# A selective scan on one core: the low half of the x-projection split moves from VectorE to GpSimd

## The chip, the cores and the metric

One Trainium2 chip, one core. The metric is the device time of one execution, in microseconds (us), and smaller is better. TensorE multiplies matrices into the banks of the accumulator memory (PSUM), ScalarE and VectorE read and write both PSUM and the state memory (SBUF), GpSimd reads and writes SBUF only, and SyncE issues the transfers. In the rows the engines are PE (matmul), PEld (weight load), DVE (VectorE), ACT (ScalarE), POOL (GpSimd) and SP (SyncE).

## What is computed

Two layers over x of 8 images, 192 channels and 64 by 64 positions. The second is a non-local attention block, which the change leaves alone. The first, cut to what matters:

```python
xn = _ln_cf(x, ln_w, ln_b)
xc, z = jnp.split(jnp.einsum('dc,bchw->bdhw', in_proj_w, xn), 2, axis=1)
xc = silu(depthwise_conv3x3(xc) + conv_b)
xs = four orders of xc: by rows, by columns, and both reversed      # K = 4
x_dbl = jnp.einsum('kcd,bkdl->bkcl', x_proj_w, xs)                  # 12 + 4 + 4 = 20 rows
dts, Bv, Cv = jnp.split(x_dbl, [R, R + N], axis=2)
dt = softplus(jnp.einsum('kdr,bkrl->bkdl', dt_proj_w, dts) + dt_proj_b)
h[t] = exp(dt[t] * A) * h[t-1] + dt[t] * Bv[t] * u[t]               # 4 states a channel
y[t] = sum over states of h[t] * Cv[t]                              # + Ds * xs
```

The 20 rows of x_dbl are dt's 12 inputs, 4 rows of B and 4 of C. All is float32.

## The kernel before

The loop `b` over the 8 images holds four stages with a barrier behind each: project, scan, mix, attend. Only the scan stage is touched. It cuts each of the four orders k into 8 chunks of 512 positions, so an image has 32 chunks, which the code counts with g (over all images, 32 an image). Orders 0 and 2 read u along rows, orders 1 and 3 read it with a stride of 64 elements. Every engine has its own instruction stream and its own function `body` for one chunk; the order is written out by hand, the functions called in `body(g)` work for chunks g, g+1 and g+2 at once, and semaphores join the engines. The sets `xhl`, `dt` and `bs` are double (par is g modulo 2); the eight PSUM banks `ps` are single.

For one chunk, in the order in which the data flow:

- `xdbl` (TensorE, L381 to L386) computes x_dbl into bank 0. The weights hold the 20 columns twice, so that rows 0 to 19 and rows 32 to 51 of the bank are the same 20 rows. It waits for `xlo_ready` of the chunk before, since it overwrites bank 0.
- `copy_xd` (ScalarE, L709) copies rows 0 to 19 of bank 0 to `xd` in SBUF. From there `dtproj` (TensorE, L392) computes dt's input into banks 6 and 7, and SyncE saves the B rows and broadcasts them to `bs` (L293 to L299).
- `copy_high` (ScalarE, L715) rounds rows 0 to 63 of bank 0 to the narrower matmul format (fp32r) into `xhl[par]`. It waits until `spread` is through with the old content of that set.
- `low_half` (VectorE, L1064 to L1067) subtracts that rounded value from the exact one, in rows 32 to 63, and puts the rest in `xhl[par]`: one matmul with 64 rows then adds the high and the low half. `spread` (TensorE, L403) is that matmul; it spreads the C rows over the partitions into banks 4 and 5.
- Softplus of dt's input: five ScalarE operations (`soft_abs` to `soft_log`), `residue` on VectorE (L1072), `residue` on GpSimd (L927, dt plus ze), and `softplus` on VectorE (L1078), which waits for GpSimd's `sp_ready`.
- `times_u` (GpSimd, two operations at L933) forms du = dt * u, and `drive` (GpSimd, L942) forms dbu = bs * du, in three operations q = 0, 1, 2 of two scans each.
- For each q, `scans` (VectorE, L1088, two scans of 512 steps, whose decay ScalarE has put in banks 2 and 3) and `times_c` (VectorE, L1096, h times the spread C rows). TensorE adds the products up in bank 1 (`sum_first`, `sum_second`, `sum_rest`).

VectorE's stream for one chunk is: scans 0, times_c 0, softplus(g+1), scans 1, times_c 1, scans 2, times_c 2, low_half(g+2), residue(g+2). GpSimd's is: residue(g+1), times_u(g+1), drive 0, drive 1 and drive 2 of g+1. Ahead of the first `body` of an image a prologue does the first two chunks' steps.

Of the kernel before, what the change touches and what calls it, by code (L numbers as in the profile page):

```python
# [19 lines left out]
F32 = mybir.dt.float32  # L20
F32R = mybir.dt.float32r
ALU = mybir.AluOpType
ACT = mybir.ActivationFunctionType
# [4 lines left out]
P = 128  # L28
R = C - P
# [5 lines left out]
NX = RANK + 2 * NS  # L35
NT = NS + NS // 2
NP = NT // 2
LO = 32
# [12 lines left out]
def build(nc, nb, x, vec, w_in, w_x, w_dt, sel, fold, ident, w_out, w_att, gb, w_w, out):  # L51
# [3 lines left out]
    with ctx:  # L55
# [96 lines left out]
        xd = sb("xd", [P, T], where=scx)  # L152
# [17 lines left out]
        mark = sem("mark")  # L170
# [464 lines left out]
        def _(act):  # L635
# [10 lines left out]
            with act.Fori(0, nb) as b:  # L646
# [58 lines left out]
                def copy_xd(g):  # L705
                    act.wait_ge(S["xdbl_ready"], g + 1)
                    act.wait_ge(S["dtpre_ready"], g + 1)
                    act.wait_ge(S["rows_saved"], g * 16 + 16)
                    A(xd[0:NX, :], ps[0:NX, 0, :], ACT.Copy).then_inc(S["xd_ready"], 1)  # L709

                def copy_high(par, g):


                    act.wait_ge(S["cbc_ready"], g * NP + 1)
                    A(xhl[par][0:64, :], ps[0:64, 0, :], ACT.Copy).then_inc(S["xhi_ready"], 1)  # L715

                def soft_abs(g):
                    act.wait_ge(S["dtpre_ready"], g + 2)
# [157 lines left out]
        @block.gpsimd  # L876
        def _(pool):
            for t in (win1[:, :], wo1[:, :], wa1[:, :], wx0[:, :], wx1[:, :], wdt[:, :], foldw[:, :], skip1[:, :], eye1[:, :], selr[:, :].bitcast(F32)):
                pool.memset(t, 0.0).then_inc(S["pads_set"], 1)
            pool.wait_ge(s_load, NL)  # L880
            pool.memset(avg[:, :], 1.0 / C)
            pool.memset(eps[:, :], 1e-5)
            pool.memset(xb[:, :, :], 0.0).then_inc(S["xb_zero"], 1)
            barrier(pool, 0, -1)

            def zero_rows(n, one, tiles):
                for t in tiles:
                    pool.memset(t, 0.0).then_inc(S["rows_zero"], 1)  # L888
                pool.wait_ge(S["rows_zero"], n)
                pool.sem_inc(mark, 1)  # L890
                pool.memset(nb_[R:R + 1, :], 1.0).then_inc(S["row_one"], 1)
                pool.wait_ge(S["row_one"], one)
                pool.sem_inc(mark, 1)

            with pool.Fori(0, nb) as b:
                zero_rows(b * 6 + 2, b * 2 + 1, (sqb[R:P, :], nb_[R:P, :]))

                for r, t in enumerate(padi):
                    for edge in (t[:, 0:1, :], t[:, PW - 1:PW, :], t[:, 1:PW - 1, 0:1], t[:, 1:PW - 1, PW - 1 - r:PW]):
                        m = pool.memset(edge, 0.0)  # L900
                        m.then_inc(S["borders_set"], 1)
                pool.memset(tapw[:, :, :], 0.0).then_inc(S["tapw_ready"], 1)
                pool.wait_ge(S["tapw_ready"], b * 19 + 1)
                pool.sem_inc(mark, 1)
                for j in range(6):
                    for r in range(1 + (j % 2 == 0)):
                        rows_ = slice(r * R, r * R + R)
                        t = V_TAP + 9 + 3 * (j // 2) + 2 * (j % 2) + r
                        for half in range(2):
                            pool.tensor_scalar(tapw[rows_, j, half * R:half * R + R], foldw[rows_, R:P], vecs[rows_, t:t + 1],  # L910
                                               None, ALU.mult).then_inc(S["tapw_ready"], 1)


                def step(c, par, which):
                    if "u" in which:
                        w = b * NCH + (c - 3)
                        pool.wait_ge(S["cs_ready"], w * 3 + 3)
                        sl = bass.ds((c - 3) * T, T)
                        pool.tensor_tensor(u[:, :, sl], u[:, :, sl], cs[:, :, :], ALU.mult).then_inc(S["u_ready"], 1)
                run_project(pool, step)  # L920
                barrier(pool, b, 0)


                def residue(par, g):

                    pool.wait_ge(S["soft_ready"], g * 5 + 5)
                    pool.tensor_tensor(dt[par][:, :, :], dt[par][:, :, :], ze[:, :, :], ALU.add).then_inc(S["sp_ready"], 1)  # L927

                def times_u(k, c, par, g):
                    pool.wait_ge(S["dt_ready"], g + 2)  # L930
                    pool.wait_ge(S["dbu_ready"], g * NP + 4)
                    for r in range(2):
                        m = pool.tensor_tensor(flat(du[:, r, :]), flat(dt[par][:, r, :]), chunk(u[:, r], c, k % 2), ALU.mult)  # L933
                        m.then_inc(S["du_ready"], 1)
                    pool.wait_ge(S["du_ready"], g * 2 + 4)

                def drive(q, s, par, g):
                    if q == 0:
                        pool.wait_ge(S[f"b_loaded{par}"], (g - par) * 24 + 48)
                    pool.wait_ge(S["scan_link"], s * 2 + 2)  # L940
                    r = 0 if 2 * q < NS else 1
                    pool.tensor_tensor(dbu[:, q, :, :], bs[par][:, q, :, :],  # L942
                                       du[:, r:r + 1, :].to_broadcast([P, 2, T]), ALU.mult).then_inc(S["dbu_ready"], 1)

                def body(k, par, g, before, now, nxt, after):
                    if nxt:
                        residue(1 - par, g + 1)
                        times_u(*nxt, 1 - par, g + 1)
                        for q in range(NP):
                            drive(q, (g + 1) * NP + q, 1 - par, g + 1)  # L950
                g_0 = b * G
                residue(0, g_0)
                times_u(0, 0, 0, g_0)
                for q in range(NP):
                    drive(q, g_0 * NP + q, 0, g_0)
                run_chunks(pool, b, body)
                barrier(pool, b, 1)


                zero_rows(b * 6 + 6, b * 2 + 2, (yt[R:P, :, :], sqb[R:P, :], nb_[R:P, :], ob[R:P, :]))  # L960
                pool.memset(xb[R:P, :, :], 0.0).then_inc(S["xb_zero"], 1)
                pool.wait_ge(S["xb_zero"], b + 2)
                pool.sem_inc(mark, 1)
                for n, (t, v) in enumerate(((phh[O:O + 1, :], 1.0), (phl[O:O + 1, :], 0.0), (gth[:, :, O:O + 1], 1.0),
                                            (gtl[:, :, O:O + 1], 0.0))):
                    pool.memset(t.bitcast(F32), v).then_inc(S["att_set"], 1)
                    pool.wait_ge(S["att_set"], b * 4 + (n + 1))
                    pool.sem_inc(mark, 1)
                barrier(pool, b, 2)
                barrier(pool, b, 3)  # L970
# [3 lines left out]
        def _(dve):  # L974
# [29 lines left out]
            with dve.Fori(0, nb) as b:  # L1004
# [52 lines left out]
                dve.memset(xd[:, :], 1.0).then_inc(S["zero_h"], 1)  # L1057
                dve.memset(h[:, :, T - 1:T], 0.0).then_inc(S["zero_h"], 1)
                for t in xhl:
                    dve.memset(t[R:P, :].bitcast(F32), 0.0).then_inc(S["zero_h"], 1)  # L1060
                dve.wait_ge(S["zero_h"], b * (K + 3) + 4)
                dve.sem_inc(S["scan_set"], 1)

                def low_half(par, g):  # L1064
                    dve.wait_ge(S["xhi_ready"], g + 1)
                    TT(xhl[par][LO:LO + 32, :], ps[LO:LO + 32, 0, :], xhl[par][LO:LO + 32, :].bitcast(F32),
                       ALU.subtract).then_inc(S["xlo_ready"], 1)  # L1067

                def residue(g):

# [27 lines left out]
                def body(k, par, g, before, now, nxt, after):  # L1098
                    for q in range(NP):
                        s = g * NP + q  # L1100
                        scans(k, q, s)
                        times_c(q, s)
                        if q == 0 and nxt:

                            softplus(1 - par, g + 1)
                    if after:
                        low_half(par, g + 2)
                        residue(g + 2)
                    if nxt and nxt[0] != k:

                        end = T - 1 if nxt[0] < 2 else 0
                        dve.wait_ge(S["hc_ready"], g * NP + (NP + 3))
                        dve.sem_inc(mark, 1)
                        dve.memset(h[:, :, end:end + 1], 0.0).then_inc(S["zero_h"], 1)  # L1114
                        dve.wait_ge(S["zero_h"], b * (K + 3) + (k + 5))
                        dve.sem_inc(mark, 1)
                g_0 = b * G
                low_half(0, g_0)
                residue(g_0)
                softplus(0, g_0)  # L1120
                low_half(1, g_0 + 1)
                residue(g_0 + 1)
                run_chunks(dve, b, body)
                barrier(dve, b, 1)
# [208 lines left out]
```

## Time and profile before

| What | Value |
|---|---|
| median of 3 runs | 10093.42 us (10088.11 to 10101.04) |
| the profiled execution's own time | 10092.67 us |
| its span, first to last instruction | 10090.8 us |
| busy: PE, DVE, ACT, POOL | 9260.9, 7541.6, 6270.0, 3449.7 us |
| granted TensorE clock, mean | 0.963 |

The span is one profiled execution; 1.87 us of the execution's time lie outside it. Busy time is the time in which an engine had an instruction running; a share of it over the whole span mixes four stages. A row of a timeline gives start, length, engine, line, operation, output and inputs, how many instructions it merges, and in brackets the engine's idle time ahead of it with what ended it. The length of merged instructions runs from the first start to the last end.

### The profile page before, as it was taken

To read this page: it belongs to the slowest core of one execution; us is meant where nothing else is said; L and a number is where in the kernel's file an instruction comes from. 1 tells how busy PE (TensorE), PEld (TensorE's weight loads), DVE (VectorE), ACT (ScalarE), POOL (GpSimd) and SP (SyncE) were. 2 spreads that over 40 slices of the span, in tenths; PEclk is the share of its full clock that TensorE was granted. 3 is DMA by queue.
4 is the path that set the end of the run, shared out by engine and by line. 5 is a ranking of instruction groups with operands and counts; after the bars stand their busy time and mean duration, and the time that the engine had idled before them with its cause. 6 is when DMAs were issued, how large, how long until landed. Compare 5 with 4: busy or idle time off the path is not lost.

```text
span 10090.8 us, 108759 instructions
## 1 busy us (share of the span) xinstructions
PE 9260.9 (92%) x28420; PEld 4969.4 (49%) x28420; DVE 7541.6 (75%) x8593; ACT 6270.0 (62%) x7748; POOL 3449.7 (34%) x1937
## 2 busy tenths in 40 slices
PE   7999989999899998999979999899998999989999
PEld 3336733367333663336633366333663336633366
DVE  6976669766697666976669766697667976679766
ACT  6755667556675556755567555675556755567555
POOL 3850038400484004840048400484004840048400
PEclk9999989999899998999999999899998999999999
DMA  1320013200131001310013100131001310013100
GB/s 57 110 67 7 8 56 107 63 8 6 56 107 63 8 6 56 107 63 8 6 56 108 62 8 6 61 108 57 8 6 62 107 57 8 7 62 107 57 8 8
DMA packets 159892, 488.46 MB, mean 48 GB/s; under 512 B 21721, under 2 KB 22713, under 8 KB 126606
## 3 DMA queue, kind: packets, MB, share of 16 engines
q1 hardware_dynamic: 159374, 482.72, 15.1%
q8 instruction: 182, 2.98, 0.1%
q14 instruction: 336, 2.75, 0.1%
HBM read 455.38 MB, written 27.26 MB: 48 GB/s over the span
## 4 chain that ended last, share of the span: by engine, by line
PE 66%; DVE 14%; issue 13%; ACT 3%; POOL 2%; DVEq 1%; SPq 0%; ACTq 0%; POOLq 0%; DMA 0%
DVE h L1088 7%; PE ps L546 5%; PE ps L559 5%; PE ps L547 5%; PE ps L548 5%; PE ps L561 5%; PE ps L560 5%; PE ps L469 4%; PE ps L430 3%; PE ps L392 2%; PE ps L427 2%; PE ps L384 2%; PE ps L411 2%; PE ps L414 2%; PE ps L328 2%
## 5 line engine op out<-in xcount | busy, mean ns | idle before, releaser
L1213 DVE TENSOR_TENSOR pl<-pf,ph 128x1024 fp32r<-128x1024 f32 x1024 | 1254.7, 1225 | 1215.5 <-ACT ph L868 1214.4
L1088 DVE TENSOR_TENSOR_SCAN h<-ps,h,dbu 128x512 f32<-128x512 f32 x1536 | 1884.5, 1268 | 18.7 <-DVE h L1114 5.3
L942 POOL TENSOR_TENSOR dbu<-bs,du 128x1024 f32<-128x1024 f32 x768 | 1799.0, 2372 | 52.8 <-POOL du L933 52.8
L868 ACT ACTIVATE ph<-pf 128x1024 fp32r<-128x1024 f32 x1024 | 1085.3, 1060 | 830.7 <-PE ps L561 830.4
L888 POOL MEMSET sqb<- 64x512 f32 x16 | 8.3, 519 | 4271.9 <-issue 4267.0
L860 ACT ACTIVATE pf<-ps 128x1024 f32<-128x1024 f32 x1024 | 1051.1, 1026 | 651.4 <-PE ps L548 651.4
L742 ACT ACTIVATE ps<-dt,negA 128x512 f32<-128x512 f32 x1536 | 1033.0, 684 | 439.7 <-DVE h L1088 404.8
L1197 DVE TENSOR_REDUCE mx<-ps 128x1 f32<-128x512 f32 x1792 | 1165.1, 684 | 69.3 <-PE ps L469 41.8
L1096 DVE TENSOR_TENSOR hc<-h,ps 128x1024 f32<-128x1024 f32 x768 | 937.9, 1221 | 190.8 <-PE ps L403 110.4
L933 POOL TENSOR_TENSOR du<-dt,u 128x512 f32<-128x512 f32 x512 | 706.7, 1402 | 623.4 <-DVE dt L1078 623.4
L559 PE MATMUL ps<-ph,gth 128*97 128x512 f32 x2048 | 817.1, 399 | 80.8 <-ACT yraw L848 72.1
L546 PE MATMUL ps<-thc,phh 97*128 97x512 f32 x2048 | 867.3, 423 | 6.7 <-ACT thc L843 6.7
L547 PE MATMUL ps<-thc,phl 97*128 97x512 f32 x2048 | 819.6, 400 | 0.0
L548 PE MATMUL ps<-thc,phh 97*128 97x512 f32 x2048 | 817.0, 399 | 0.0
L561 PE MATMUL ps<-pl,gth 128*97 128x512 f32 x2048 | 809.9, 395 | 0.0
L560 PE MATMUL ps<-ph,gtl 128*97 128x512 f32 x2048 | 808.3, 395 | 0.0
L403 PE MATMUL ps<-xhl,selr 128*128 128x512 f32 x1536 | 693.4, 532 | 124.2 <-DVE hc L1096 124.2
L469 PE MATMUL ps<-phh,thc 96*128 96x512 f32 x1824 | 617.4, 405 | 30.0 <-POOLq L176 18.8
L927 POOL TENSOR_TENSOR dt<-dt,ze 128x1024 f32<-128x1024 f32 x256 | 604.8, 2363 | 97.3 <-ACT dt L735 97.3
L392 PE MATMUL ps<-xd,wdt 128*128 128x512 f32 x1024 | 515.0, 627 | 100.8 <-DVE dt L1078 93.8
L403 PEld LDWEIGHTS ps<-xhl,selr 128*128 128x128 f32 x1536 | 265.8, 190 | 587.2 <-DVE hc L1096 378.1
L1021 DVE SCALAR_TENSOR_TENSOR u<-pad,vecs,u 128x512 f32<-128x512 f32 (+1 forms) x512 | 490.9, 960 | 61.5 <-DVE db L1009 18.8
(188 smaller groups left out, 16077.4 us busy)
## 6 DMA issues: line engine op xcount, KB each, us to landing
bs<-rows SPq DMA_DIRECT2D x256, 1024.0 KB, 5.2
bs<-rows SPq DMA_DIRECT2D x512, 256.0 KB, 6.1
xa<-in_x SPq DMA_DIRECT2D x130, 256.0 KB, 2.9
xb<-in_x SPq DMA_DIRECT2D x130, 128.0 KB, 3.0
out<-fa SPq DMA_DIRECT2D x64, 256.0 KB, 2.0
out<-fa SPq DMA_DIRECT2D x64, 128.0 KB, 2.3
rows<-xd SPq DMA_DIRECT2D x256, 8.0 KB
gate<-in_sel SPq DMA_DIRECT2D x1, 384.0 KB
```

What stands on the lines that cost most here:

```text
L546: mm(dst, kk, thc[par][0][:, :], start=True, stop=False)
L547: mm(dst, phl[:, m * P:(m + 1) * P], thc[par][0][:, :], start=False, stop=False)
L548: q = mm(dst, kk, thc[par][1][:, :], start=False, stop=True)
L559: mm(dst, gth[:, m, :], ph[:, mp % 2, e, :], start=(m == 0), stop=False)
L560: mm(dst, gtl[:, m, :], ph[:, mp % 2, e, :], start=False, stop=False)
L561: q = mm(dst, gth[:, m, :], pl[:, mp % 2, e, :], start=False, stop=(m == MT - 1))
L860: A(pf[:, mp % 2, :, :], ps[:, 2 * (mp % 2):2 * (mp % 2) + 2, :], ACT.Exp)\
L868: A(ph[:, mp % 2, :, :], pf[:, mp % 2, :, :], ACT.Copy).then_inc(S["ph_ready"], 1)
L942: pool.tensor_tensor(dbu[:, q, :, :], bs[par][:, q, :, :], du[:, r:r + 1, :].to_broadcast([P, 2, T]), ALU.mult).then_inc(S["dbu_ready"], 1)
L1088: dve.tensor_tensor_scan(h[:, j, ::step], ps[:, 2 + e, ::step], dbu[:, q, e, ::step], h[:, j, end:end + 1], ALU.mult, ALU.add)\
L1197: dve.tensor_reduce(mx[:, t, m:m + 1], ps[:, 5 + j % 2, :], AX.X, ALU.max)\
L1213: TT(pl[:, mp % 2, :, :], pf[:, mp % 2, :, :], ph[:, mp % 2, :, :].bitcast(F32), ALU.subtract)\
```

## The change

The low half moves from VectorE to GpSimd. GpSimd cannot read bank 0, so it subtracts the rounded rows 0 to 19 of `xhl[par]` from `xd`, the copy of the same rows in SBUF, and writes rows 32 to 51. `copy_high` rounds only 32 rows. ScalarE's `copy_xd` waits for one thing more, that the low half of the chunk before has read `xd`. In GpSimd's stream the low half of chunk g+2 stands between drive 1 and drive 2 of chunk g+1, with a wait for drive 1 to end ahead of it and a wait for its own end behind it. In the prologue, the low half of chunk 0 is GpSimd's first step, and that of chunk 1 comes behind all three drives of chunk 0. VectorE's memset of `xhl` covers all 128 rows, in place of rows 64 to 127.

```diff
@@ ScalarE
                     act.wait_ge(S["rows_saved"], g * 16 + 16)
+                    act.wait_ge(S["xlo_ready"], g + 1)
                     A(xd[0:NX, :], ps[0:NX, 0, :], ACT.Copy).then_inc(S["xd_ready"], 1)
...
-                    A(xhl[par][0:64, :], ps[0:64, 0, :], ACT.Copy).then_inc(S["xhi_ready"], 1)
+                    A(xhl[par][0:LO, :], ps[0:LO, 0, :], ACT.Copy).then_inc(S["xhi_ready"], 1)
@@ GpSimd
+                def low_half(par, g):
+                    pool.wait_ge(S["xhi_ready"], g + 1)
+                    pool.tensor_tensor(xhl[par][LO:LO + NX, :], xd[0:NX, :], xhl[par][0:NX, :].bitcast(F32), ALU.subtract)\
+                        .then_inc(S["xlo_ready"], 1)
+                    pool.wait_ge(S["xlo_ready"], g + 2)
+                    pool.sem_inc(mark, 1)
...
                         for q in range(NP):
                             drive(q, (g + 1) * NP + q, 1 - par, g + 1)
+                            if after and q == 1:
+                                pool.wait_ge(S["dbu_ready"], (g + 1) * NP + 6)
+                                low_half(par, g + 2)
                 g_0 = b * G
+                low_half(0, g_0)
                 residue(0, g_0)
                 times_u(0, 0, 0, g_0)
                 for q in range(NP):
                     drive(q, g_0 * NP + q, 0, g_0)
+                pool.wait_ge(S["dbu_ready"], g_0 * NP + 7)
+                low_half(1, g_0 + 1)
@@ VectorE
                 for t in xhl:
-                    dve.memset(t[R:P, :].bitcast(F32), 0.0).then_inc(S["zero_h"], 1)
+                    dve.memset(t[:, :].bitcast(F32), 0.0).then_inc(S["zero_h"], 1)
...
-                def low_half(par, g):
-                    dve.wait_ge(S["xhi_ready"], g + 1)
-                    TT(xhl[par][LO:LO + 32, :], ps[LO:LO + 32, 0, :], xhl[par][LO:LO + 32, :].bitcast(F32),
-                       ALU.subtract).then_inc(S["xlo_ready"], 1)
...
                     if after:
-                        low_half(par, g + 2)
                         residue(g + 2)
...
-                low_half(0, g_0)
                 residue(g_0)
                 softplus(0, g_0)
-                low_half(1, g_0 + 1)
                 residue(g_0 + 1)
```

## Rows read from the trace of the kernel before

**Rows 1.** Busy time by stretch: image 0's scan stage, its start, strided chunks, unstrided.

```profile
core 0: us, PE busy (x) PEld busy (x) DVE busy (x) ACT busy (x) POOL busy (x), PEclk, DMA share, GB/s
...
165.00:655.00 490.00, 450.48 (x952) 176.12 (x953) 445.65 (x391) 355.82 (x478) 387.40 (x192) 0.98 0.33 104
...
180.00:210.00 30.00, 21.89 (x42) 8.49 (x43) 21.83 (x20) 19.11 (x26) 24.45 (x13) 0.79 0.32 109
...
330.00:360.00 30.00, 30.00 (x60) 10.99 (x59) 27.06 (x25) 22.36 (x31) 24.03 (x13) 1.00 0.31 103
...
480.00:510.00 30.00, 26.05 (x63) 10.73 (x61) 29.04 (x26) 22.69 (x32) 24.93 (x13) 1.00 0.33 106
```

**Rows 2.** Timeline, unstrided chunk (order 2), GpSimd's and VectorE's steps around softplus.

```profile
483.65 2.37 POOL L927 TENSOR_TENSOR dt<-dt,ze 128x1024 f32<-128x1024 f32 x1
...
486.92 1.22 DVE L1078 SCALAR_TENSOR_TENSOR dt<-ps,dt 128x1024 f32<-128x1024 f32 x1
...
488.31 2.49 POOL L933 TENSOR_TENSOR du<-dt,u 128x512 f32<-128x512 f32 x2 [2.29 <-DVE dt L1078]
...
490.96 7.04 POOL L942 TENSOR_TENSOR dbu<-bs,du 128x1024 f32<-128x1024 f32 x3 [0.17 <-POOL du L933]
...
495.59 0.68 DVE L1066 TENSOR_TENSOR xhl<-ps,xhl 32x512 fp32r<-32x512 f32 x1
...
496.32 0.30 PEld L384 LDWEIGHTS ps<-u,wx 128*128 128x128 f32 x2 [0.42 <-DVE xhl L1066]
...
497.94 2.37 POOL L927 TENSOR_TENSOR dt<-dt,ze 128x1024 f32<-128x1024 f32 x1
...
501.29 1.22 DVE L1078 SCALAR_TENSOR_TENSOR dt<-ps,dt 128x1024 f32<-128x1024 f32 x1
```

**Rows 3.** Timeline, strided chunk (order 1), the same steps and TensorE's.

```profile
339.90 3.02 POOL L933 TENSOR_TENSOR du<-dt,u 128x512 f32<-128x512 f32 x2 [2.73 <-DVE dt L1078]
...
346.78 0.59 ACT L715 ACTIVATE xhl<-ps 64x512 fp32r<-64x512 f32 x1 [0.40 <-PE ps L403]
...
346.94 1.22 DVE L1096 TENSOR_TENSOR hc<-h,ps 128x1024 f32<-128x1024 f32 x1 [1.12 <-PE ps L403]
...
348.93 0.30 PEld L384 LDWEIGHTS ps<-u,wx 128*128 128x128 f32 x2 [0.42 <-DVE xhl L1066]
...
350.08 2.37 POOL L927 TENSOR_TENSOR dt<-dt,ze 128x1024 f32<-128x1024 f32 x1
...
353.89 1.22 DVE L1078 SCALAR_TENSOR_TENSOR dt<-ps,dt 128x1024 f32<-128x1024 f32 x1
```

**Rows 4.** Timeline, prologue of image 0's scan: softplus alone, TensorE restarting.

```profile
176.49 2.34 POOL L927 TENSOR_TENSOR dt<-dt,ze 128x1024 f32<-128x1024 f32 x1 [11.85 <-ACT dt L735]
...
178.93 1.22 DVE L1078 SCALAR_TENSOR_TENSOR dt<-ps,dt 128x1024 f32<-128x1024 f32 x1 [2.23 <-POOL dt L927]
...
188.21 2.07 PE L384 MATMUL ps<-u,wx 128*128 128x512 f32 x2 [4.16 <-DVE xhl L1066]
```

**Rows 5.** Costliest groups, whole execution: the scans, GpSimd's drives and du.

```profile
L1088 DVE TENSOR_TENSOR_SCAN h<-ps,h,dbu 128x512 f32<-128x512 f32 x1536 | 1884.5, 1268 | 18.7 <-DVE h L1114 5.3
L942 POOL TENSOR_TENSOR dbu<-bs,du 128x1024 f32<-128x1024 f32 x768 | 1799.0, 2372 | 52.8 <-POOL du L933 52.8
...
L933 POOL TENSOR_TENSOR du<-dt,u 128x512 f32<-128x512 f32 x512 | 706.7, 1402 | 623.4 <-DVE dt L1078 623.4
```

**Rows 6.** Tile du, 450 to 515 us: durations min/median/max in ns.

```profile
L942 POOL TENSOR_TENSOR dbu<-bs,du x15: 2357/2374/2384, 447.9 to 510.1; 128x1024 f32<-128x1024 f32 x15
L933 POOL TENSOR_TENSOR du<-dt,u x8: 1267/1268/1277, 459.6 to 503.9; 128x512 f32<-128x512 f32 x8
```

**Rows 7.** GpSimd's groups by shape: few elements, few partitions (busy us, mean ns).

```profile
L910 POOL TENSOR_SCALAR tapw<-foldw,vecs 64x64 f32<-64x64 f32 x144 | 66.6, 473 | 8.7 <-POOL tapw L902 2.2
...
L891 POOL MEMSET nb<- 1x512 f32 x16 | 8.3, 517 | 2.5 <-POOL nb L888 1.2 <-POOL ob L888 1.2
...
L879 POOL MEMSET wx<- 128x512 f32 x2 | 1.0, 527 | 0.0
```

## The prediction, made before the changed kernel was run

> **What bounds the kernel now.** I read the busy times by stretch first, to find the stage that the change touches; then the timelines of one chunk of each kind, to find the loop that sets the pace; then the groups of GpSimd, for prices.
>
> The scan stage of an image lasts about 490 us [rows 1] of the 1261 that are an eighth of the span. Over the whole span GpSimd looks almost free (34% busy, in the table of the profile), but nearly all of that lies in this stage: 387.4 of 490 us here, 24 to 25 of every 30 us in mid-stage. That is the first thing to see: the engine that takes the work on has about 5 us in 30 left.
>
> The pace has two forms [rows 1]. In unstrided chunks VectorE is busy 29.04 of 30 us and is the bound: from one softplus to the next there are 501.29 − 486.92 = 14.37 us [rows 2]. In most strided chunks TensorE is busy 30.00 of 30 us, a chunk lasts 353.89 − 338.51 = 15.38 us (softplus to softplus; the first one starts 1.22 + 0.17 us ahead of the du at 339.90, as the next paragraph has it [rows 3]), and VectorE waits 1.12 us for `spread` ahead of the last times_c. In both, `xdbl` of the next chunk starts when VectorE's low half ends (idle 0.42, released by L1066) [rows 2, 3].
>
> What decides here is a third loop, which is not yet the bound. GpSimd's du waits for softplus; softplus waits for GpSimd's residue; and residue stands behind GpSimd's three drives, which stand behind du. So the idle time of 2.29 us ahead of du [rows 2] is mostly not free. Where nothing else is in the way, in the prologue, residue ends at 176.49 + 2.34 = 178.83 and softplus starts 0.10 us later, at 178.93 [rows 4]; it lasts 1.22 us; and du starts 0.17 us after it ends, 488.31 against 488.14 [rows 2]. These 1.49 us of GpSimd's idle time are the loop itself. Only the rest is slack: 2.29 − 1.49 = 0.80 us in that chunk; in the strided one residue ends at 352.45 and softplus starts at 353.89, which is 1.44 − 0.10 = 1.34 us [rows 3]. For all chunks together: du was waited for 623.4 us in 256 chunks [rows 5]; the first of each image waits for softplus alone, 1.49 us, which leaves 611.5 us over 248 chunks, 2.47 each, and a slack of 2.47 − 1.49 = 0.98 us.
>
> **The change, part by part.**
>
> *VectorE's operation goes*: 0.68 us a chunk [rows 2]. In unstrided chunks that alone would bring the pace from 14.37 to 13.69 us. In strided ones VectorE waits anyway, so nothing.
>
> *GpSimd's operation comes*: one per chunk, 20x512 with two inputs. The trace has no such shape. Nearest is du in unstrided chunks, same engine, two float32 inputs, 512 elements a row: 1.27 us [rows 6]. That it has 20 partitions and not 128 should not help: a memset of 1x512 lasts 517 ns and one of 128x512 527 ns [rows 7]. The ends: below, the 64x64 operation at 0.47 us [rows 7], as if few rows were cheap; above, the 1024-element operation at 2.37 us [rows 6], as if reading rows 0 to 19 and writing rows 32 to 51 cost a second pass. I take 1.27 us, since the row has the same number of elements and inputs.
>
> *Its two waits come*: the one on drive 1 ahead of it and the one on itself behind it. A wait of GpSimd for its own last operation is in the trace, between du and drive 0: 52.8 us in 256 chunks, 0.21 us each [rows 5]. Without a wait its operations run over each other by about 0.05 us: three drives of 2.37 us take 7.04, and residue begins 0.06 us before the last ends [rows 2]. Insertion: 1.27 + 2 × 0.21 + 0.05 = 1.74 us a chunk. What is queued behind is drive 2, then residue, and softplus waits for that. The ends of the insertion are 0.94 and 2.84 us.
>
> *Where it lands*: all of it lies in the third loop. That loop is now 14.37 − 0.80 = 13.57 us (unstrided) and 15.38 − 1.34 = 14.04 us (strided); with 1.74 us more it is 15.31 and 15.78 us, above both 14.37 and 15.38. So GpSimd becomes the bound everywhere, VectorE stands idle ahead of softplus, and the 0.68 us that it gave up is lost in that.
>
> *The other waits*: TensorE's xdbl now waits for GpSimd. Softplus to the end of the low half is 1.22 + 0.17 + 3.19 (du and the wait) + 4.69 (two drives) + 0.21 + 1.27 = 10.75 us in a strided chunk; before, xdbl began 348.93 − 338.51 = 10.42 us after softplus. Ahead of the next softplus that leaves TensorE 15.38 − 10.42 = 4.96 us before and 15.78 − 10.75 = 5.03 after, so I cost it at nothing: the longer chunk covers it. Without that cover it would cost at most these 0.33 us. ScalarE's new wait in `copy_xd` asks for the low half that xdbl, just ahead of it, has waited for already: nothing. `copy_high` ends about 0.4 us before drive 1 (at 347.37, against 339.90 + 3.19 + 4.69 = 347.78) [rows 3], so GpSimd doesn't wait for it. The memset and the fewer rows of copy_high: nothing, by the memsets of rows 7 (time goes by the elements of a row).
>
> *The prologue*: the low half of chunk 1 comes behind the drives, as much as in a chunk; I count that insertion among the 248. It also holds up xdbl of chunk 2, which began at 188.21 [rows 4], to about 191.5. The granted clock is 0.79 from 180 to 210 us and 1.00 later [rows 1], so part of that stretch, after TensorE's wait, is at the lower level of 1.2 GHz; the first pair of xdbl lasts 2.07 us there [rows 4]. I take nothing for it, since GpSimd sets the pace there too, and as bounds 0 to 4 us an image (xdbl's two pairs at 2.07 once more): 0 to 32 us in all.
>
> *A rule weighed.* The fifteen drives of that stretch last 2357 to 2384 ns [rows 6], though VectorE's scans, which read h and dbu from SBUF, run beside some of their parts and not others; so no operation of one holds up the other by more than 0.03 us. The Trainium skill (SBUF — State Buffer, section Who interferes with whom) says that a VectorE instruction with two SBUF inputs and a GpSimd instruction that reads SBUF exclude each other for a whole instruction. By that rule, if a scan counts as one, the low half could stand behind it. The rows speak against it.
>
> **The sum.** 248 × (1.74 − 0.98) = 188 us. The profiled execution took 10092.67 us (span 10090.8, and 1.87 around it), 0.75 below the median of the runs shown, so the forecast is 10092.67 + 188 = 10281 us, 1.9% slower.
>
> **The rivals.**
>
> *Faster: the idle time is free.* Were GpSimd's whole 2.47 us slack, 1.74 would fit, and VectorE would gain 0.68 us in the unstrided half (about 15 of 31 chunks an image): 8 × 15 × 0.68 = 82 us, 10011 us. For it: VectorE is the bound there, and GpSimd idles 5 us in 30. Against: softplus begins only 0.80 us after it could. The point from which it decides is an insertion under about 0.8 us, with prices near the 0.47 row and waits that vanish. Chance 0.06.
>
> *No change: a cheap low half.* At 0.47 us the insertion is 0.94, near the mean slack of 0.98: unstrided chunks lose 0.14 us, in strided ones GpSimd could be done at 347.78 + 0.21 + 0.47 = 348.46, ahead of xdbl's 348.93 [rows 3], of which TensorE, busy all the time, can use little; I allow 0.17. Together 120 × 0.14 = 17 us more to 120 × 0.17 = 20 less: about 10093. Chance 0.07.
>
> *Much slower.* Either the shift between partitions doubles the price (insertion 2.84: 248 × 1.86 = 461 us, 10554), chance 0.04; or a scan of VectorE's and the low half exclude each other, and it stands behind one for its 1.27 us in every chunk [rows 5] (248 × 1.27 = 315 us more, 10596), chance 0.03. The rule weighed above is one that would do this.
>
> *The clock.* If TensorE, waiting longer for GpSimd, lost its higher level for part of each scan stage, a few more matmul pairs of 2.07 us would come on top [rows 4]. Against: where TensorE is busy 26.05 of 30 us, the clock is 1.00 all the same [rows 1]. Five such pairs an image, some 10 us, give about 10361. Chance 0.05.
>
> **How the numbers follow.** The forecast keeps 0.75: GpSimd's loop with an insertion of 1.35 to 2.2 us, 10185 to 10395 us. The range runs from 10175 to 10400 and takes in the clock rival; the three outer ones, 0.20 together, are left out. Within 0.2% (20 us) of no change is about what a measurement of this kernel can tell: faster 0.06, same 0.07, slower 0.87.
>
> **What would show it.** Right: GpSimd busy over 27 of 30 us in mid-stage; softplus waiting for GpSimd's residue in every chunk; unstrided chunks at 15.2 to 15.4 us, strided at 15.7 to 15.9; du waiting 1.5 us. The GpSimd subtraction at 1.2 to 1.3 us with 0.2 on either side. Wrong: softplus not waiting for GpSimd, du waiting over 1.6 us, or a subtraction under 0.5 us.

## The result and the profile after

The changed kernel is slower, as forecast: 10273.17 us (median of 4 runs, 10264.80 to 10274.52) against 10095.44 us of the kernel before (4 runs, 10088.11 to 10101.04), a ratio of 1.0175 with a 95% interval of 1.0157 to 1.0192. The forecast was 10281 us, or 1.019 times the profiled execution of the kernel before.

The busy times of the changed kernel by stretch: image 0's scan stage, then a stretch of strided chunks, then one of unstrided chunks (columns as in [rows 1]).

```profile
165.00:680.00 515.00, 450.19 (x946) 179.13 (x947) 423.79 (x358) 351.76 (x478) 431.14 (x225) 0.96 0.31 99
340.00:370.00 30.00, 29.55 (x58) 10.58 (x57) 25.17 (x22) 21.42 (x29) 25.91 (x14) 1.00 0.30 87
490.00:520.00 30.00, 24.26 (x60) 10.56 (x59) 26.00 (x22) 21.07 (x30) 25.62 (x15) 1.00 0.33 106
```

Against [rows 1], VectorE falls from 29.04 to 26.00 of 30 us in the unstrided stretch, and GpSimd rises only from 24.93 to 25.62. An engine that bounds the work and yet is busy for only 25.62 of 30 us looks odd. The rest is its waits in the loop, which the timeline of one unstrided chunk shows (it answers to [rows 2]; `...` marks rows left out):

```profile
506.82 1.23 DVE L1088 SCALAR_TENSOR_TENSOR dt<-ps,dt 128x1024 f32<-128x1024 f32 x1 [1.90 <-POOL dt L936]
...
508.22 2.50 POOL L942 TENSOR_TENSOR du<-dt,u 128x512 f32<-128x512 f32 x2 [1.50 <-DVE dt L1088]
...
510.89 4.71 POOL L951 TENSOR_TENSOR dbu<-bs,du 128x1024 f32<-128x1024 f32 x2 [0.16 <-POOL du L942]
...
515.67 1.27 POOL L928 TENSOR_TENSOR xhl<-xd,xhl 20x512 fp32r<-20x512 f32 x1
...
517.00 1.12 PE L384 MATMUL ps<-u,wx 128*128 128x512 f32 x2 [0.74 <-POOL xhl L928]
...
517.21 2.35 POOL L951 TENSOR_TENSOR dbu<-bs,du 128x1024 f32<-128x1024 f32 x1 [0.26 <-POOL xhl L928]
...
519.52 2.35 POOL L936 TENSOR_TENSOR dt<-dt,ze 128x1024 f32<-128x1024 f32 x1
...
521.98 1.23 DVE L1088 SCALAR_TENSOR_TENSOR dt<-ps,dt 128x1024 f32<-128x1024 f32 x1 [1.53 <-POOL dt L936]
```

Read from softplus at 506.82 to softplus at 521.98, every step begins when the one ahead of it in the loop ends: 15.16 us, where it was 14.37 [rows 2]. VectorE, which had no idle time ahead of softplus, now waits 1.53 us there for GpSimd's residue; du waits 1.50 us, the bare loop. The strided chunk, against [rows 3]:

```profile
337.45 3.03 POOL L942 TENSOR_TENSOR du<-dt,u 128x512 f32<-128x512 f32 x2 [1.50 <-DVE dt L1088]
...
353.23 3.04 POOL L942 TENSOR_TENSOR du<-dt,u 128x512 f32<-128x512 f32 x2 [1.50 <-DVE dt L1088]
```

15.78 us from du to du, and again only the 1.50 us. Waits of VectorE and GpSimd by what ended them, from 205 to 640 us (sum in us, times, longest), in two answers, and behind them GpSimd's wait ahead of du over the whole execution:

```profile
DVE dt L1088 <- POOL dt L936: 34.4, 28, 1.9
```

```profile
POOL du L942 <- DVE dt L1088: 42.3, 28, 1.8
POOL dbu L951 <- POOL xhl L928: 7.6, 28, 0.6
```

```profile
POOL du L942 <- DVE dt L1088: 386.3, 256, 1.8
```

386.3 / 256 = 1.51 us, where it was 623.4 / 256 = 2.44 [rows 5]; the shortest single wait of the 256 is 1.50 us. So the slack, 0.98 us in the mean, is used up in every chunk. A tempting other reading stands in the view of the tile xhl, whole execution (who waited for its writers; and the low half's duration, min/median/max ns):

```profile
L928 POOL TENSOR_TENSOR xhl<-xd,xhl x256: 1254/1272/1287, 172.1 to 9618.8; 20x512 fp32r<-20x512 f32 x128
...
PEld ps L384: 325.0, 240
```

TensorE's weight load for xdbl waited 325.0 us for the low half: by far the longest wait on the moved operation, and larger than the loss. In the same view of the kernel before, where it waited for VectorE's low half, it is

```profile
PEld ps L384: 142.5, 240
```

The wait grew by 182.5 us, as much as the whole loss. That is the rival which the experiments must exclude.

**Where the 182 us lie.** The profiled executions took 10274.52 and 10092.67 us, 181.9 apart. Measured from VectorE's first memset of the scan stage to its first one of the mix stage, the eight scan stages make 176.9 of it (4173.0 against 3996.1 us). Of these, 172.9 lie between the first and the last softplus of each image (31 intervals), 5.8 in the prologue ahead of the first, and −1.9 behind the last. The other 5.0 us lie in the stages that the change leaves alone; runs of one kernel differ by as much.

### The profile page after: what moved, and what is told of

It reads as the page before. It is cut to its first block, busy times and chain, and to the rows that moved or that the text cites. A ratio compares the mean times of both kernels' runs of the same rounds, so it can differ in the third digit from the quotient of the medians.

```text
span 10272.5 us, 109775 instructions
## 1 busy us (share of the span) xinstructions
PE 9257.8 (90%) x28420; PEld 4991.2 (49%) x28420; DVE 7379.0 (72%) x8337; ACT 6239.0 (61%) x7748; POOL 3786.4 (37%) x2193
## 3 DMA queue, kind: packets, MB, share of 16 engines
q14 instruction: 344, 2.82, 0.1%
## 4 chain that ended last, share of the span: by engine, by line
PE 50%; POOL 21%; issue 17%; DVE 8%; ACT 3%; POOLq 1%; DVEq 0%; SPq 0%; ACTq 0%; DMA 0%
POOL dbu L951 9%; POOL dt L936 5%; PE ps L546 5%; PE ps L559 5%; PE ps L547 5%; PE ps L548 5%; PE ps L561 5%; PE ps L560 5%; PE ps L469 4%; POOL du L942 3%; POOL xhl L928 3%; DVE dt L1088 3%; PE ps L328 2%; PE ps L329 2%; PE ps L346 2%
## 5 line engine op out<-in xcount | busy, mean ns | idle before, releaser
L942 POOL TENSOR_TENSOR du<-dt,u 128x512 f32<-128x512 f32 x512 | 707.6, 1405 | 386.3 <-DVE dt L1088 386.3
L403 PE MATMUL ps<-xhl,selr 128*128 128x512 f32 x1536 | 720.3, 550 | 66.5 <-DVE hc L1106 64.6
L384 PE MATMUL ps<-u,wx 128*128 128x512 f32 x512 | 410.1, 887 | 283.0 <-POOL xhl L928 211.2
```

## The experiments

The theory: GpSimd's loop (softplus, du, drives, low half, residue, softplus) is the bound after the change, and had 0.8 to 1.3 us of slack before it. The rivals: TensorE's wait for the low half costs the time; or GpSimd's idle time before was free; or the operands decide (SBUF copies in place of the bank). Each ratio is to the kernel before in runs made beside the experiment: 10099.90 us for experiments 1, 2, the second kernel of 3 and the first of 4, and 10098.59 us for the others.

**1. xdbl no longer waits for the low half** (changed kernel; `xhi_ready` starts at 1, and GpSimd's wait on it counts one more).

```diff
-                    pe.wait_ge(S["xlo_ready"], g + 1)
+                    pe.wait_ge(S["xhi_ready"], g + 1)
                     order = k % 2
```

> The changed kernel, but TensorE's xdbl waits only until copy_high has read bank 0 (xhi_ready), not for GpSimd's low half; nothing else reads the bank now. If GpSimd's loop (du, drives, low half, residue, softplus) is the bound, nothing changes: 10270 us, 15 either way, although TensorE's biggest wait of the changed kernel (325 us for the low half ahead of xdbl) disappears. If that wait is what costs, the time goes back to about 10095 us or below.

Measured: 10269.87 us, ratio to before 1.0159 (1.0129 to 1.0190). TensorE's wait is gone; of it remain the prologues:

```profile
PEld ps L384: 40.0, 8
```

(who waited for the writers of xhl, whole execution, first kernel of the experiments.) And xdbl begins as the low half begins:

```profile
500.70 1.27 POOL L928 TENSOR_TENSOR xhl<-xd,xhl 20x512 fp32r<-20x512 f32 x1 [0.16 <-POOL dbu L951]
500.74 0.42 PEld L384 LDWEIGHTS ps<-u,wx 128*128 128x128 f32 x2
```

285 of the 325 us were taken away and nothing came back: the wait stood in the shadow of GpSimd's loop.

**2. The insertion without its waits.** The low half is written over the rounded rows 0 to 19, and rows 32 to 51 keep the rounded ones; the matmul's selection weights are the same for both, so the sum stays what it was. The operation then reads and writes the same rows. In the changed kernel it writes rows 32 to 51 from rows 0 to 19, and has a wait on either side. The Trainium skill (GPSIMD Engine Reference, section Instruction dispatch) says that GpSimd's cores hold 16 partitions each and that a following instruction is no barrier between them; no run here shows that. Whether the changed kernel needs its two waits for that reason is not shown either.

```diff
-                    A(xhl[par][0:LO, :], ps[0:LO, 0, :], ACT.Copy)
+                    A(xhl[par][0:64, :], ps[0:64, 0, :], ACT.Copy)
...
-                    pool.tensor_tensor(xhl[par][LO:LO + NX, :], xd[0:NX, :], ...
+                    pool.tensor_tensor(xhl[par][0:NX, :], xd[0:NX, :], ...
-                    pool.wait_ge(S["xlo_ready"], g + 2)
-                    pool.sem_inc(mark, 1)
...
-                                pool.wait_ge(S["dbu_ready"], (g + 1) * NP + 6)
```

> The changed kernel with the low half written in place: copy_high rounds 64 rows again, and GpSimd puts the rest into rows 0 to 19, where it also reads; rows 32 to 51 keep the rounded values. The two waits around it go. If the loop of GpSimd is the bound, the insertion falls from 1.66 us (after) to 1.27 less the 0.05 of overlap, 1.22: 248 chunks by 0.44 us, 109 us less, about 10165 us. If the held-up xdbl is the bound, xdbl starts only 0.07 us earlier and the time stays within 20 us of 10273.

Measured: 10155.96 us, ratio 1.0052 (1.0039 to 1.0064): 117 us less than the changed kernel. GpSimd's timeline in an unstrided chunk:

```profile
510.19 4.70 POOL L949 TENSOR_TENSOR dbu<-bs,du 128x1024 f32<-128x1024 f32 x2 [0.25 <-POOL du L940]
514.85 1.27 POOL L928 TENSOR_TENSOR xhl<-xd,xhl 20x512 fp32r<-20x512 f32 x1
516.09 2.36 POOL L949 TENSOR_TENSOR dbu<-bs,du 128x1024 f32<-128x1024 f32 x1
```

Start to start, the low half now takes 516.09 − 514.85 = 1.24 us, and the chunk 14.80 us in place of 15.23 (mean of the first seven intervals behind the first, all images). The operation itself lasts 1.27 us as before, so what went is the two waits: they were two thirds of the loss.

**3. More work for GpSimd, nothing else.** Once in the kernel before, once in the changed one; nobody reads `spare`. To make room for it the weights of xdbl lie 64 columns apart and not 128 (rows 64 to 127 of bank 0, which nobody reads, get other values).

```diff
+   pool.tensor_tensor(spare[0:NX, :], wdt[0:NX, 0:T], wdt[0:NX, T:2 * T], ALU.subtract)
```

In the kernel before, between drive 1 and drive 2:

> The kernel before with one more GpSimd operation a chunk that nobody reads or waits for, 20x512 with two inputs, between drive 1 and drive 2; VectorE keeps its low half. If GpSimd's idle time ahead of du is mostly the loop (0.80 us of slack in an unstrided chunk, 1.34 in a strided one), the 1.22 us stick out: unstrided 13.57 + 1.22 = 14.79 us for 14.37, the five longest strided chunks of an order unchanged at 15.38, the others about 15.26; 10145 to 10170 us. If the idle time (2.47 us a chunk) is free, the operation is hidden: 10093 us.

Measured: 10155.07 us, 1.0053 (1.0037 to 1.0070). Two successive du of an unstrided stretch:

```profile
509.24 2.50 POOL L934 TENSOR_TENSOR du<-dt,u 128x512 f32<-128x512 f32 x2 [1.50 <-DVE dt L1085]
...
524.06 2.50 POOL L934 TENSOR_TENSOR du<-dt,u 128x512 f32<-128x512 f32 x2 [1.50 <-DVE dt L1085]
```

14.82 us, for the 14.79 of the slack: idle time that looked like 2.29 us could not take 1.22. The result is within 1 us of experiment 2, where VectorE's operation is gone and the low half moved, and most unstrided chunks take 14.71 to 14.82 us in both. With an insertion of the same size, whether VectorE still does its low half makes no difference.

In the changed kernel, between drive 2 and residue:

> The changed kernel with one more GpSimd operation a chunk that nobody reads, 20x512 with two inputs, between drive 2 and residue, so behind the low half that xdbl waits for. If the loop of GpSimd is the bound, its 1.22 us (1.27 less the overlap) comes in full: 240 chunks, 293 us, about 10565 us. If xdbl's wait for the low half is the bound, the operation is hidden and the time stays near 10273 us.

Measured: 10544.76 us, 1.0429 (1.0397 to 1.0460), 272 us more than the changed kernel (293 were expected). The operation stands behind the low half, so it cannot delay the xdbl that waits for that; it costs its whole length all the same (chunks of 16.48 for 15.23 us).

**4. The low half in the idle time.** In GpSimd's stream it stands between residue and du, where 1.49 us are spent on waiting for softplus; in place as in experiment 2, `xd` double (the weights of xdbl closer together, to make room), xdbl waiting as in experiment 1.

```diff
                         residue(1 - par, g + 1)
+                        low_half(1 - par, g + 1)
                         times_u(*nxt, 1 - par, g + 1)
...
-                            if after and q == 1:
-                                pool.wait_ge(S["dbu_ready"], (g + 1) * NP + 6)
-                                low_half(par, g + 2)
```

> GpSimd does the low half of chunk g+1 between residue and du of chunk g+1, where it stands idle for 1.49 us because of softplus, in place as in e2_samerows and without waits; xd is double, and xdbl waits for copy_high alone. If GpSimd's loop was the bound and the idle time there is free, the 1.27 us cost next to nothing, the unstrided chunks become bound by VectorE without its operation (13.69 us for 14.37, 82 us less than before the change) and the strided ones by TensorE (15.38 or up to 0.3 us less): 9980 to 10020 us. If the move off VectorE gains nothing by itself, about 10093 us.

Measured: 9992.54 us, 0.9884 (0.9854 to 0.9913), faster than both kernels. The timeline, unstrided:

```profile
482.02 1.23 DVE L1083 SCALAR_TENSOR_TENSOR dt<-ps,dt 128x1024 f32<-128x1024 f32 x1
...
493.07 2.35 POOL L934 TENSOR_TENSOR dt<-dt,ze 128x1024 f32<-128x1024 f32 x1
495.39 1.27 POOL L928 TENSOR_TENSOR xhl<-xd,xhl 20x512 fp32r<-20x512 f32 x1
...
495.58 1.22 DVE L1083 SCALAR_TENSOR_TENSOR dt<-ps,dt 128x1024 f32<-128x1024 f32 x1
...
496.96 2.49 POOL L940 TENSOR_TENSOR du<-dt,u 128x512 f32<-128x512 f32 x2 [0.30 <-DVE dt L1083]
```

The low half runs beside softplus, du waits 0.30 us and not 1.50, and a chunk takes 495.58 − 482.02 = 13.56 us. The gain lies mainly in the unstrided chunks (13.55 to 13.60 us in most of them, for 14.37; the longest strided ones mostly 15.20 to 15.22, for 15.38). Freeing xdbl is not what gives it there: with xdbl freed and the operation left on VectorE, most unstrided chunks take 14.24 to 14.56 us (second kernel of experiment 5). So the idea of the change (work off VectorE, where that is the bound) is worth about 100 us; its place in GpSimd's stream, with the waits there, made it a loss.

The same with xdbl held by the low half:

```diff
-                    pe.wait_ge(S["xhi_ready"], g + 1)
+                    pe.wait_ge(S["xlo_ready"], g + 2)
```

> As e4_gap, but xdbl of chunk g+2 waits again for GpSimd's low half of chunk g+1, which in this place ends about 5 us later relative to softplus than xdbl began. TensorE's chain from xdbl over spread, copy_high, the last softplus steps, residue and the low half to the next xdbl then is the bound, 13.2 + 0.6 + 2.1 + 2.4 + 1.3 and latencies, near 20 us in strided chunks: 10500 to 11100 us. If xdbl's wait for the low half costs nothing wherever it stands, about 9993 us as e4_gap.

Measured: 11103.81 us, 1.0995 (1.0977 to 1.1013), just above the stated range; strided chunks take 19.4 us in the mean. The mean granted clock also fell, to 0.912 from 0.963; what that adds was not measured. The view of waits, 205 to 640 us, and rows of a strided chunk:

```profile
PEld ps L384 <- POOL xhl L928: 106.8, 23, 4.8
PE ps L384 <- POOL xhl L928: 96.9, 23, 4.4
```

```profile
338.27 1.25 POOL L928 TENSOR_TENSOR xhl<-xd,xhl 20x512 fp32r<-20x512 f32 x1
...
339.58 1.97 PE L384 MATMUL ps<-u,wx 128*128 128x512 f32 x2 [4.35 <-POOL xhl L928]
...
340.29 1.22 DVE L1083 SCALAR_TENSOR_TENSOR dt<-ps,dt 128x1024 f32<-128x1024 f32 x1
```

So TensorE's wait for the low half is not harmless as such. In the changed kernel it is covered because the low half ends well ahead of the next softplus (516.94 against 521.98 us in the rows above). Here it ends 0.77 us ahead of it, TensorE waits up to 4.4 us for it, and that decides. Experiment 4 needs both: the idle place and the freed xdbl.

**5. The operands alone.** The kernel before, VectorE's low half in its old place, from `xd` and rows 0 to 19 of `xhl` (with the change's `copy_xd`, `copy_high` and memset); first with xdbl waiting for it, then for copy_high.

```diff
-                    TT(xhl[par][LO:LO + 32, :], ps[LO:LO + 32, 0, :], xhl[par][LO:LO + 32, :].bitcast(F32),
+                    TT(xhl[par][LO:LO + NX, :], xd[0:NX, :], xhl[par][0:NX, :].bitcast(F32),
                        ALU.subtract).then_inc(S["xlo_ready"], 1)
```

> The kernel before, with VectorE's low half in its old place, but reading what the changed kernel reads: xd and the rounded rows 0 to 19, two SBUF inputs; xdbl waits for it as before. If VectorE and GpSimd do not hold each other up, 0.6 to 0.7 us for the subtraction and 10095 us, 20 either way. If an operation with two SBUF inputs and a GpSimd operation exclude each other, the subtraction stands behind drives of up to 2.37 us: it lasts well over 0.7 us or starts late, and unstrided chunks, where VectorE is the bound, grow by up to some 1 us: 10100 to 10350 us.

> As e5_dve, and xdbl waits only for copy_high. Unstrided chunks stay bound by VectorE (14.37 us); in strided ones TensorE starts xdbl up to 0.7 us earlier, of which a part counts: 10060 to 10095 us without exclusion. With exclusion as in e5_dve, less the same part.

Measured: 10226.46 us, 1.0129 (1.0112 to 1.0146), and 10121.38 us, 1.0018 (1.0008 to 1.0028). The case with exclusion came out in both, though not where it was expected: unstrided chunks did not grow (14.25 to 14.27 us in most of them, for 14.37), while the longest strided ones did (17.04 to 17.13, for 15.38). First of the two kernels, tile xhl:

```profile
L1067 DVE TENSOR_TENSOR xhl<-xd,xhl x256: 680/792/2864, 168.6 to 9566.5; 20x512 fp32r<-20x512 f32 x128
```

and a strided chunk of it:

```profile
343.39 7.02 POOL L943 TENSOR_TENSOR dbu<-bs,du 128x1024 f32<-128x1024 f32 x3 [0.17 <-POOL du L934]
...
348.61 2.34 DVE L1067 TENSOR_TENSOR xhl<-xd,xhl 20x512 fp32r<-20x512 f32 x1
...
350.36 2.82 POOL L928 TENSOR_TENSOR dt<-dt,ze 128x1024 f32<-128x1024 f32 x1
```

With the bank as one input the operation lasted 0.68 us [rows 2]. Here it starts at 348.61, in the middle of drive 2, and ends at 350.95, about 0.54 us after the drives' end at 350.41; residue behind it is stretched from 2.37 to 2.82 us. In the profile such a hold-up is not idle time but a longer operation. It is the same in all 125 cases of this trace in which the operation starts with more than 0.3 us of a GpSimd operation to go: it ends 0.54 to 0.55 us after that one. In most unstrided chunks it starts as a drive ends, lasts 0.68 to 0.73 us, and the next drive pays:

```profile
497.68 7.51 POOL L943 TENSOR_TENSOR dbu<-bs,du 128x1024 f32<-128x1024 f32 x3 [0.17 <-POOL du L934]
...
502.29 0.68 DVE L1067 TENSOR_TENSOR xhl<-xd,xhl 20x512 fp32r<-20x512 f32 x1
```

Three drives take 7.51 us here and 7.04 in [rows 2]. So VectorE can't simply take the copies as its inputs either, beside a busy GpSimd.

## Why the prediction was right

**The loop.** Right, and nearly the whole of the loss (172.9 of 181.9 us). Unstrided chunks were forecast at 15.31 us and take 15.15 and 15.24 us in turn; strided ones at 15.78 and take 15.70 to 15.80. Experiments 1, 2 and 3 each change one thing about it: freeing TensorE gives nothing, a shorter insertion gives its length back, and one more operation costs its length. In experiment 4 the operation, without its waits and with xdbl freed, fits into the bare loop's idle time.

**The slack.** 0.80 us in an unstrided chunk: an insertion of 1.22 us that nobody reads gave 14.82 us for 14.79 (experiment 3). Right.

**The price of the operation.** 1.27 us taken from du's row, 1.272 us the median of 256. The shift between partitions and the 20 rows change nothing.

**The price of its waits.** The term that was off. I took 0.21 us for each, from the wait between du and drive 0. Measured: 515.67 − (510.89 + 4.71) = 0.07 us ahead, 0.26 us behind. The insertion was 1.66 and not 1.74 us: 248 × 0.08 = 20 us too much. Two chunks of each image are about 0.3 us longer than the others of their kind (once a wait of 0.56 us behind the low half); why was not looked into. 248 × (1.66 − 0.98) + 16 × 0.3 = 173 us, which is what the intervals show. That the whole, 181.9 us, came so near the forecast 188 is in part luck: the 20 us too much stand against these longer chunks, the prologue and the 5.0 us outside the scan stages, none of which the sum had.

**The prologue.** Costed at nothing, with 0 to 32 us as bounds. It took 5.8 us in all, nearly all of it in three images, where TensorE ran dtproj of chunk 0 at the lower level: four matmuls in 3.78 us in image 0, at a granted clock of 0.50, which is 1.2 GHz (1.98 us at 1.00 in the kernel before). Seven of the eight experiments' kernels show it too, in one to three images each and not always the same, and one in none; whether the change makes it likelier is not shown. The delayed xdbl of chunk 2 cost nothing that shows: the first softplus interval is 15.13 us in every image, GpSimd's loop.

**xdbl's wait and copy_high.** Costed at nothing; experiment 1 confirms it for xdbl, and GpSimd waited for copy_high only in the prologues (8 waits in the view of the tile xhl). That xdbl's wait depends on the place, experiment 4 shows (11103.81 us).

**The rule weighed.** A scan and GpSimd's low half do not exclude each other: the low half lasts 1254 to 1287 ns over all 256, and the scans that overlap it (136 cases, by up to 0.69 us) last 1257 to 1285 ns. The rule itself holds here where it clearly applies, an operation of VectorE's with two whole SBUF tensors as inputs (experiment 5: up to 2.86 us for 0.68). The Trainium skill (SBUF — State Buffer, section Who interferes with whom) says that the second to start is blocked for the whole instruction of the first; the 2.34 us above, which end behind the drive, agree.

**The rivals.** "The idle time is free" and "a cheap low half" fell with the first profile (1.27 us, du waiting 1.50 us), and the doubled price with it. The clock stayed at 1.00 in both stretches above; over the whole execution the granted mean is 0.958 for 0.963, and since du waits no longer than the bare loop nearly everywhere, it does not set the pace.

**The signs.** One that I named did not come: GpSimd is busy for 25.62 and 25.91 of 30 us, not over 27. It contradicted my own loop: a chunk of 15.31 us with 1.49 us of idle time ahead of du and three waits of 0.21 us gives 25.8 of 30.

## What to carry to other kernels

An engine's idle time is not room: subtract what the loop through the other engines needs (here 1.49 of 2.29 us), and only the rest can take work. When work moves to another engine, put it where that engine waits for the loop, not between two steps of it; the same operation cost 182 us in one place and, with its waits and its consumer's wait removed, gained about 100 in the other. A long wait in a trace says nothing of its price until the wait is taken away.

## What was not expected of the hardware

A wait of GpSimd on its own last operation cost 0.07 us ahead of the low half (0.16 us in experiment 1) and 0.26 us behind it, against 0.21 us between du and drive; without waits successive operations overlap by 0.03 to 0.05 us (1.27 us long, 1.24 apart). Removing the two waits around one 20x512 operation was worth 117 of 178 us. And an operation on 20 partitions of VectorE, with both inputs in SBUF, excluded GpSimd's 128-partition operations as a whole: 680 to 2864 ns for the same work, and drives of 2.82 us in the median where they started beside it, for 2.37 us otherwise.
